# L2_ca in a four-layer cross-attention kernel: paired scores, sums of exps on GpSimd, and a later wait for them

## Chip, cores and metric

One core of a Trainium2 chip runs the whole program. The metric is device time in microseconds, the median of several runs; lower is better.

## What is computed

Four transformer layers in float32 over x (8 batches of 112 tokens, 256 channels) with a context of 8 x 375 tokens. The blocks, in order: L0 self-attention, cross-attention and a mixture of experts; L1 self-attention, MLP, cross-attention, MLP; L2 cross-attention, gated MLP, self-attention, gated MLP; L3 cross-attention with rotary positions, MLP. The change touches one of them, L2's cross-attention. It has 16 query heads and 4 key/value heads of 64 channels, and normalises queries and keys:

```python
xn = rmsnorm(x, s1)
q = einsum('btc,chd->bthd', xn, wq_c)
k = einsum('btc,chd->bthd', ctx, wk_c)
v = einsum('btc,chd->bthd', ctx, wv_c)
q, k = qk_norm(q), qk_norm(k)          # each head's row divided by its root mean square
k, v = repeat(k, 4, axis=2), repeat(v, 4, axis=2)
attn = softmax(einsum('bqhd,bkhd->bhqk', q, k) / 8)
out = einsum('bhqk,bkhd->bqhd', attn, v)
x = x + out.reshape(B, T, H * D) @ wo_c
```

## The kernel before

Each engine runs its own program; they meet at semaphores. A block is a loop over the 8 batches (`batches`: body(0), a hardware loop over 1 to 6, body(7), and body(8), which finishes what lags). While batch b's attention is computed, the same body prepares batch b+1. The order on every engine is written out by hand: `SCHEDULES["L2_ca"]` says at which of 12 steps each piece of preparation stands.

The block L2_ca (`keys_first`) puts keys on the partitions. A batch has 4 groups of 4 query heads, one group to a key/value head; the 375 keys lie in 3 chunks of 125. So there are 12 scores (`units`), each a matmul of 125 keys by 448 (4 heads x 112 queries), L873. Two key/value heads share the 128 rows of kT, and each group's queries are held twice the height, with zeros in the other head's 64 rows (`qz`, written by ScalarE in two copies with a mask, L1264). ScalarE takes exp of each score (L1277) into pT. Because keys are on the partitions, softmax's sum over keys is a matmul with ones: VectorE first adds the three chunks of a group (`add_chunks`, L1698 for the first two, L1702 for the third; 8 additions a batch), then PE multiplies by ones (L933). `weigh` handles two groups at a time, twice a batch: it waits for the sums, does 6 matmuls of exps by values (L927, side by side in two column halves) and 2 with ones. VectorE takes the reciprocal (L1707) and multiplies (L1709); PE projects (`project`, L947) once both halves are there; VectorE adds to X (L1719).

PE's pieces for the next batch, by step: 0 CT0, CT1 (context transposed); 1 XT, KP0 (keys, L816); 2 KP1; 3 QP0 (queries, L821); 4 QP1; 5 V0; 6 V1; 8 QT0 (queries transposed, L828); 9 QT1, KT1 (L835); 10 KT0. They share two PSUM banks, 7 and 5, in turn, so each waits until ScalarE has copied the piece before last. The projection uses bank 7 too and so waits for KP1's copy (L1256). `weigh` stands at step 7 (groups 0, 1) and at step 1 of the next batch (groups 2, 3), `project` at step 3. Scores rotate through 4 banks: a score waits for the exp of the score four before.

VectorE, between QP1 and QT0: the square of the queries (L1605), its sum by head (L1607), 12 small operations for reciprocal roots, the scaling of queries (L1622) and of keys (L1625), which releases QT0. The additions of chunks stand in the same queue one step behind their scores. In the last batch VectorE also computes, in small operations spread over the steps, the statistics that the next MLP needs, and after it normalises six batches of tokens (L1512). GpSimd does nothing in this block; behind it in its queue stands the splitting of weights for the MLP (`split_weights`, L2073 to L2079).

## Time and profile before

| | |
|---|---|
| median of 3 runs | 2048.26 us (2045.43 to 2050.31) |
| profiled execution, its time | 2057.58 us |
| its span | 2055.8 us |
| mean granted PE clock | 0.932 |
| PE busy | 1776.4 us, 86% |
| VectorE (DVE) busy | 1332.9 us, 65% |
| ScalarE (ACT) busy | 866.2 us, 42% |
| GpSimd (POOL) busy | 629.1 us, 31% |

A busy share is an average over 13 blocks with different limits. A float32 matmul appears as two instructions, so a score is "x2" and a pair of scores "x4". Matmuls are pipelined: the start of the next one, rather than the end of a row, tells how long PE was taken.

### The profile page before, as it was taken

To read this page: it belongs to the slowest core of one execution; us is meant where nothing else is said; L and a number is where in the kernel's file an instruction comes from. 1 tells how busy PE (TensorE), PEld (TensorE's weight loads), DVE (VectorE), ACT (ScalarE), POOL (GpSimd) and SP (SyncE) were. 2 spreads that over 40 slices of the span, in tenths; PEclk is the share of its full clock that TensorE was granted. 3 is DMA by queue.
4 is the path that set the end of the run, shared out by engine and by line. 5 is a ranking of instruction groups with operands and counts; after the bars stand their busy time and mean duration, and the time that the engine had idled before them with its cause. 6 is when DMAs were issued, how large, how long until landed. Compare 5 with 4: busy or idle time off the path is not lost.

```text
span 2055.8 us, 34270 instructions
## 1 busy us (share of the span) xinstructions
PE 1776.4 (86%) x10630; PEld 1237.2 (60%) x10630; DVE 1332.9 (65%) x3354; ACT 866.2 (42%) x2513; POOL 629.1 (31%) x732
## 2 busy tenths in 40 slices
PE   5969999769996878988779999896888979898988
PEld 4746665558985656655565555483444845455567
DVE  5866767301117876788666676796677966556665
ACT  3735554322334643565324444342332435444521
POOL 2325555210022234676320000130000325455534
PEclk9979998879998978999789999997998989999999
DMA  4100000468862000002100010101000100000200
GB/s 167 37 20 15 13 7 16 147 217 301 307 236 82 0 1 31 32 30 71 67 8 16 16 69 0 42 11 62 0 0 19 55 1 12 23 11 11 72 1 18
DMA packets 36627, 115.15 MB, mean 56 GB/s; under 512 B 2961, under 2 KB 23345, under 8 KB 29345
## 3 DMA queue, kind: packets, MB, share of 16 engines
q1 hardware_dynamic: 33968, 107.33, 15.2%
q0 software_dynamic: 2544, 6.43, 1.0%
q8 instruction: 56, 0.92, 0.2%
q14 instruction: 59, 0.48, 0.1%
HBM read 99.34 MB, written 14.40 MB: 55 GB/s over the span
## 4 chain that ended last, share of the span: by engine, by line
PE 44%; issue 20%; DVE 14%; POOL 14%; ACT 4%; DMA 3%; SPq 1%; POOLq 0%; DVEq 0%; ACTq 0%
POOL arena L2020 11%; PE ps L1008 7%; PE ps L1048 4%; PE ps L821 4%; PE ps L873 3%; PE ps L1168 3%; PE ps L1152 3%; PE ps L927 3%; PE ps L816 3%; PE ps L947 2%; PE ps L891 1%; PE ps L863 1%; DMA wml<-in_wm_L_moe 1%; PE ps L933 1%; ACT arena L1286 1%
## 5 line engine op out<-in xcount | busy, mean ns | idle before, releaser
L2020 POOL TENSOR_TENSOR arena<-arena,rinv 112x375 f32<-112x375 f32 (+1 forms) x448 | 371.1, 830 | 489.9 <-DVE rinv L1675 479.7
L891 PEld LDWEIGHTS ps<-cst,arena 112*125 112x125 f32 (+1 forms) x1408 | 188.1, 184 | 176.6 <-POOL arena L2020 88.9
L891 PE MATMUL ps<-cst,arena 112*125 112x112 f32 (+1 forms) x1408 | 247.0, 294 | 45.2 <-POOL arena L2020 39.9
L1286 ACT ACTIVATE arena<-ps,negmax 112x375 f32<-112x375 f32 (+1 forms) x384 | 190.6, 501 | 168.2 <-DVE negmax L1670 167.8
L1684 DVE COPY arena<-ps 125x336 f32<-125x336 f32 x384 | 190.8, 497 | 47.3 <-PE ps L891 44.9
L2073 POOL TENSOR_TENSOR w_split_sb<-wml,w_split_sb 128x512 fp32r<-128x512 f32 (+1 forms) x40 | 45.9, 1148 | 527.0 <-ACT w_split_sb L1352 525.1
L1670 DVE TENSOR_REDUCE negmax<-ps 112x1 f32<-112x375 f32 (+1 forms) x288 | 158.3, 550 | 70.9 <-PE ps L863 61.9
L1008 PE MATMUL ps<-h_split_sb,w_split_sb 128*128 128x448 f32 x768 | 179.7, 383 | 17.8 <-DVE h_split_sb L1559 7.1
L1286 ACT ACTIVATE arena<-arena,negmax 112x112 f32<-112x112 f32 (+1 forms) x256 | 125.4, 491 | 139.1 <-DVE negmax L1659 97.0
L1008 PEld LDWEIGHTS ps<-h_split_sb,w_split_sb 128*128 128x128 f32 x768 | 150.4, 198 | 35.9 <-DVE h_split_sb L1559 13.2
L816 PE MATMUL ps<-wat,arena 128*125 128x256 f32 (+1 forms) x608 | 153.5, 390 | 16.8 <-DVE arena L1600 9.5
L816 PEld LDWEIGHTS ps<-wat,arena 128*125 128x125 f32 (+1 forms) x608 | 110.6, 189 | 46.8 <-issue 15.4
L863 PE MATMUL ps<-arena 64*112 64x375 f32 x512 | 119.0, 543 | 19.9 <-ACT arena L1286 8.6
L873 PE MATMUL ps<-arena 128*125 128x448 f32 (+1 forms) x256 | 120.6, 560 | 11.3 <-ACT arena L1268 11.3
L947 PE MATMUL ps<-wat,arena 128*112 128x256 f32 x512 | 125.2, 389 | 4.7 <-ACT arena L1294 2.9
L1707 DVE RECIPROCAL arena<-ps 128x448 f32<-128x448 f32 x32 | 94.5, 2953 | 48.4 <-PE ps L933 48.4
L1048 PE MATMUL ps<-g_split_sb,w_split_sb 128*128 128x448 f32 x480 | 113.3, 373 | 3.2 <-DVE g_split_sb L1826 3.2
L1675 DVE RECIPROCAL rinv<-rowsum 112x1 f32<-112x1 f32 (+1 forms) x448 | 70.4, 157 | 62.5 <-PE ps L868 47.3
L821 PE MATMUL ps<-wat,arena 128*112 128x512 f32 x192 | 103.2, 675 | 6.6 <-ACT arena L1224 6.5
L947 PEld LDWEIGHTS ps<-wat,arena 128*112 128x112 f32 x512 | 87.9, 179 | 32.4 <-issue 6.3
L927 PE MATMUL ps<-arena,vz 125*64 125x448 f32 (+1 forms) x448 | 98.6, 568 | 9.6 <-DVE arena L1702 6.5
L1277 ACT ACTIVATE arena<-ps 125x448 f32<-125x448 f32 (+1 forms) x128 | 70.1, 548 | 75.1 <-PE ps L873 74.8
(221 smaller groups left out, 3186.7 us busy)
## 6 DMA issues: line engine op xcount, KB each, us to landing
wml<-in_wm_L_moe SPq DMA_DIRECT2D x21, 1028.0 KB, 7.7
wml<-in_wm_L_moe SPq DMA_DIRECT2D x21, 1024.0 KB, 7.7
craw<-in_ctx SPq DMA_DIRECT2D x40, 375.0 KB
wml<-in_wm_L_m SPq DMA_DIRECT2D x3, 3072.0 KB, 13.8
wat<-in_wa_L_ca SPq DMA_DIRECT2D x2, 2560.0 KB, 10.2
wml<-in_wm_L_m SPq DMA_DIRECT2D x2, 2048.0 KB, 10.1
keys_hbm<-arena SPq DMA_DIRECT2D x8, 375.0 KB
values_hbm<-vz SPq DMA_DIRECT2D x8, 375.0 KB
```

The source lines that it names most:

```text
L816: last = mm(ps[0:blk.kp, W_BANK, i * D:(i + 1) * D], kv[:, k2, q * blk.kp:(q + 1) * blk.kp], w[:, k2], start=k2 == 0, stop=k2 == DC - 1)
L821: last = mm(ps[0:S, W_BANK, :], hT[:, k2], wq[:, k2, i * 512:(i + 1) * 512], start=k2 == 0, stop=k2 == DC - 1)
L873: mm(ps[0:blk.kp, blk.bank_at(s), 0:HG * S], kT[:, parity(b), g // 2, q * blk.kp:(q + 1) * blk.kp], qz[:, parity(b), HG * g:HG * (g + 1)], ...
L891: last = nc.tensor.transpose(ps[0:blk.kp, T_BANK + s % blk.t_banks, o:o + S], buf[:, i * blk.nk + q * blk.kp:i * blk.nk + (q + 1) * blk.kp ...
L927: last = mm(ps[64 * z:64 * z + 64, O_BANK, 0:HG * S], vz64[0:kp, par, q, (g - 1 + z) * 64:(g + z) * 64], pT[0:kp, (g - 1 + z) % 4, q], sta ...
L947: last = mm(ps[0:S, blk.out_bank, blk.out_at:blk.out_at + D], oT[:, c], wo[:, c], start=c == 0, stop=c == blk.cq - 1)
L1008: last = mm(out, w[:, k2, v], h_split_sb[:, h, k2, tokens], start=k2 == 0 and i == 0, stop=k2 == DC - 1 and i == 2)
L1048: last = mm(ACC(c, half), w[:, c * P:(c + 1) * P], g_split_sb[:, t % 2, g], start=f == 0 and i == 0, stop=f == FC - 1 and i == 2)
L1286: last = go(probs[0:S, s % blk.nprobs, i * nk:(i + 1) * nk], src[:, i * nk:(i + 1) * nk], ACT.Exp, scale=-1.0 if blk.mask == "input" else ...
L1670: v.tensor_reduce(negmax[:, s * blk.heads:(s + 1) * blk.heads], src, AX_X, ALU.max, negate=True).then_inc(maxed, 1)
L1684: last = v.tensor_copy(pT[0:kp, place(blk, s) // gu % 4, :, place(blk, s) % HG], T_[:, 0:KC * S].rearrange("p (k s) -> p k s", s=S))
L2020: pool.tensor_tensor(p3, p3, r3, ALU.mult).then_inc(scaled, 1)
```

## The change

In L2_ca alone: scores are issued in pairs, two matmuls of 64 rows each, one in the upper and one in the lower half of PE's rows, for two groups and the same chunk. Queries are kept once, scaled by 0.125, in one ScalarE copy per transposed piece instead of two. `group_of` now orders the 12 units as (group 0, chunk 0), (group 1, chunk 0), (group 0, chunk 1) and so on. The chunk additions move from VectorE's program to GpSimd's, with the same waits. `weigh` waits for the exps of its groups before its products, and for the sums just before the matmuls with ones.

```diff
-PAIRS = ("L0_ca", "L1_ca", "L3_ca",)
+PAIRS = ("L0_ca", "L1_ca", "L2_ca", "L3_ca")
...
                     if not blk.keys_first:
                         pe.wait_ge(turned, count(st["turn"], units, b, (g + 1) * gu))
-                    elif blk.kc > 1:
-
-                        pe.wait_ge(summed, count(0, 4, b, g + 1))
                     else:
-                        pe.wait_ge(exped, count(st["unit"], units, b, g + 1))
+                        pe.wait_ge(exped, count(st["unit"], units, b, (g + 1) * gu))
...
                     if blk.keys_first:
+                        if blk.kc > 1:
+                            pe.wait_ge(summed, count(0, 4, b, g + 1))
                         for z in range(2):
...
@@ VectorE @@
-                def add_chunks(b, s):
...
-                        elif at and blk.kc > 1:
-                            add_chunks(*at)
...
@@ GpSimd @@
+                def add_chunks(b, s):
+
+                    g, q = group_of(blk, s)
+                    if q == 0:
+                        return
+                    pool.wait_ge(exped, count(st["unit"], units, b, s + 1))
+                    new = pT[0:kp, g, q].rearrange("p h s -> p (h s)")
+                    if q == 1:
+                        wait(pool, av_done, count(st["group"], 2, b, g // 2 - 1))
+                        pool.tensor_tensor(psums[0:kp, g], pT[0:kp, g, 0].rearrange("p h s -> p (h s)"), new, ALU.add)\
+                            .then_inc(part_summed, 1)
+                    else:
+                        pool.wait_ge(part_summed, count(0, 4, b, g + 1))
+                        pool.tensor_tensor(psums[0:kp, g], psums[0:kp, g], new, ALU.add).then_inc(summed, 1)
+
+                def body_of_sums(b):
+                    for s in steps(b, blk, 1):
+                        at = lagged(b, s, 1, units)
+                        if at:
+                            add_chunks(*at)
...
+                elif blk.kc > 1:
+                    batches(pool, body_of_sums)
```

The order on PE around the projection, before: the second weighing's end (L933), XT (L786), KP0 (L816), score 2 (L873), KP1 (L816), score 3, then the projection (L947).

```order
L933 MATMUL ps<-arena,cst 64x448 x2
...
L786 MATMUL ps<-cst,xn 128x112
...
L816 MATMUL ps<-wat,arena 125x256 x3
...
L873 MATMUL ps<-arena 125x448 [waits exped]
...
L816 MATMUL ps<-wat,arena 125x256 [waits w_done1,w_done0]
L816 MATMUL ps<-wat,arena 125x256
...
L873 MATMUL ps<-arena 125x448 [waits exped]
...
L947 MATMUL ps<-wat,arena 112x256 [waits w_done0]
```

And now (L932 is the matmul with ones, L858 a score, L946 the projection):

```order
L932 MATMUL ps<-arena,cst 64x448 [waits summed]
L932 MATMUL ps<-arena,cst 64x448
...
L786 MATMUL ps<-cst,xn 128x112
...
L816 MATMUL ps<-wat,arena 125x256 x3
L858 MATMUL ps<-arena 125x448 [waits exped]
L858 MATMUL ps<-arena 125x448
...
L816 MATMUL ps<-wat,arena 125x256 [waits w_done1,w_done0]
L816 MATMUL ps<-wat,arena 125x256
...
L946 MATMUL ps<-wat,arena 112x256 [waits w_done0]
```

Both scores now stand before KP1, and nothing stands between KP1 and the projection.

The order on PE at a batch's end, before: score 8, QT0 (L828), score 9, QT1, KT1 (L835), score 10, KT0, score 11.

```order
L873 MATMUL ps<-arena 125x448 [waits exped]
L828 MATMUL ps<-cst,arena 128x112 [waits qk_ready,w_done1]
L828 MATMUL ps<-cst,arena 128x112 x3
L873 MATMUL ps<-arena 125x448 [waits exped]
L828 MATMUL ps<-cst,arena 128x112 [waits out_done,w_done0]
L828 MATMUL ps<-cst,arena 128x112 x3
L835 MATMUL ps<-cst,arena 128x125 [waits w_done1]
L835 MATMUL ps<-cst,arena 128x125 x2
L873 MATMUL ps<-arena 125x448 [waits exped]
L835 MATMUL ps<-cst,arena 128x125 [waits qk_ready,out_done,w_done0]
L835 MATMUL ps<-cst,arena 128x125 x2
L873 MATMUL ps<-arena 125x448 [waits exped]
```

And now:

```order
L858 MATMUL ps<-arena 125x448 [waits exped]
L858 MATMUL ps<-arena 125x448
L828 MATMUL ps<-cst,arena 128x112 [waits qk_ready,w_done1]
L828 MATMUL ps<-cst,arena 128x112 x3
L828 MATMUL ps<-cst,arena 128x112 [waits out_done,w_done0]
L828 MATMUL ps<-cst,arena 128x112 x3
L835 MATMUL ps<-cst,arena 128x125 [waits w_done1]
L835 MATMUL ps<-cst,arena 128x125 x2
L858 MATMUL ps<-arena 125x448 [waits exped]
L858 MATMUL ps<-arena 125x448
L835 MATMUL ps<-cst,arena 128x125 [waits qk_ready,out_done,w_done0]
L835 MATMUL ps<-cst,arena 128x125 x2
```

Score 9 now stands ahead of the wait for the normalised queries (qk_ready), and score 11 ahead of KT0; no score stands between QT0 and QT1, nor after KT0.

## Rows read from the trace of the kernel before

**Rows 1.** Stretch view, one batch of L2_ca: us, then busy us (instructions), granted PE clock

```profile
core 0: us, PE busy (x) PEld busy (x) DVE busy (x) ACT busy (x) POOL busy (x), PEclk, DMA share, GB/s
1131.40:1162.40 31.00, 30.71 (x127) 16.97 (x126) 21.26 (x34) 13.76 (x29) 0.00 (x0) 1.00 0.04 13
```

**Rows 2.** Timeline around QT0, PE and ACT: start us, us, engine, line, operation

```profile
1193.73 0.60 PE L828 MATMUL ps<-cst,arena 112*128 112x112 f32 x4
...
1194.37 1.16 ACT L1264 ACTIVATE arena<-ps,cst 128x448 f32<-128x448 f32 x2
...
1195.84 1.17 ACT L1264 ACTIVATE arena<-ps,cst 128x448 f32<-128x448 f32 x2
...
1196.88 0.51 ACT L1268 ACTIVATE arena<-ps 128x375 f32<-128x375 f32 x1
...
1197.44 1.89 PE L873 MATMUL ps<-arena 128*125 128x448 f32 x4
1197.67 0.53 ACT L1268 ACTIVATE arena<-ps 128x375 f32<-128x375 f32 x1
```

**Rows 3.** Timeline from the scores after KP1 to the sixth score

```profile
1207.42 0.91 PE L873 MATMUL ps<-arena 128*125 128x448 f32 x2
...
1207.62 0.39 ACT L1256 ACTIVATE arena<-ps 125x256 f32<-125x256 f32 x1 [0.32 <-PE ps L816]
...
1208.17 3.62 PE L947 MATMUL ps<-wat,arena 128*112 128x256 f32 x16
...
1215.81 0.91 PE L873 MATMUL ps<-arena 128*125 128x448 f32 x2
```

**Rows 4.** Timeline from the batch before's sixth score, VectorE's square and sum

```profile
1184.75 0.91 PE L873 MATMUL ps<-arena 128*125 128x448 f32 x2
...
1185.59 1.23 DVE L1605 TENSOR_TENSOR arena<-arena 112x1024 f32<-112x1024 f32 x1 [1.15 <-ACT arena L1253]
...
1187.02 0.63 DVE L1702 TENSOR_TENSOR arena<-arena 125x448 f32<-125x448 f32 x1 [0.21 <-DVE arena L1605]
1187.56 1.21 DVE L1607 TENSOR_REDUCE var<-arena 112x16 f32<-112x1024 f32 x1
```

**Rows 5.** Timeline of PE in L3_ca: a pair of 64 rows

```profile
1806.70 0.89 PE L868 MATMUL ps<-arena 64*112 64x375 f32 x4
1807.52 0.58 PE L891 MATMUL ps<-cst,arena 112*125 112x112 f32 x3
```

**Rows 6.** Groups of GpSimd by form: count, busy us, mean ns, idle before

```profile
L2020 POOL TENSOR_TENSOR arena<-arena,rinv 112x448 f32<-112x448 f32 x64 | 59.7, 933 | 179.2 <-DVE rinv L1675 179.2
...
L2010 POOL TENSOR_TENSOR arena<-arena,scratch 112x512 f32<-112x512 f32 x16 | 18.5, 1156 | 0.1
```

**Rows 7.** Timeline of the last batch and the tail of L2_ca

```profile
1296.48 2.96 DVE L1707 RECIPROCAL arena<-ps 128x448 f32<-128x448 f32 x1 [2.62 <-PE ps L933]
...
1300.15 1.98 PE L947 MATMUL ps<-wat,arena 128*112 128x256 f32 x8 [0.36 <-DVE arena L1709]
...
1301.97 3.17 PE L873 MATMUL ps<-arena 128*125 128x448 f32 x8
...
1305.07 2.48 PE L927 MATMUL ps<-arena,vz 125*64 125x448 f32 x12
...
1308.23 3.27 PE L873 MATMUL ps<-arena 128*125 128x448 f32 x8
...
1312.76 1.68 POOL L2073 TENSOR_TENSOR w_split_sb<-wml,w_split_sb 128x512 fp32r<-128x512 f32 x1 [268.45 <-ACT w_split_sb L1352]
1313.24 1.23 DVE L1478 TENSOR_TENSOR newton<-rstd 112x6 f32<-112x6 f32 x1
...
1317.90 2.55 DVE L1512 TENSOR_SCALAR arena<-X,rstd 112x256 f32<-112x256 f32 x6
...
1318.03 4.14 PE L927 MATMUL ps<-arena,vz 125*64 125x448 f32 x12 [6.53 <-DVE arena L1702]
...
1322.97 2.96 DVE L1707 RECIPROCAL arena<-ps 128x448 f32<-128x448 f32 x1 [2.52 <-PE ps L933]
```

**Rows 8.** Timeline of PE in L2_sa, after an idle

```profile
1541.78 1.00 PE L873 MATMUL ps<-arena 128*112 128x448 f32 x2 [1.48 <-ACT arena L1268]
```

**Rows 9.** Stretch view, 2 us of L2_sa just behind, columns as in rows 1

```profile
1544.00:1546.00 2.00, 2.00 (x6) 0.29 (x2) 0.50 (x1) 0.00 (x0) 0.00 (x0) 0.50 0.00 0
```

More of the change, by code:

```diff
@@ L1687, in copy_turned @@
                     last.then_inc(turned, 1)
-                def add_chunks(b, s):
-                    g, q = group_of(blk, s)
-                    if q == 0:
-                        return
-                    dve.wait_ge(exped, count(st["unit"], units, b, s + 1))
-                    new = pT[0:kp, g, q].rearrange("p h s -> p (h s)")
-                    if q == 1:
-                        v.tensor_tensor(psums[0:kp, g], pT[0:kp, g, 0].rearrange("p h s -> p (h s)"), new, ALU.add)\
-                            .then_inc(part_summed, 1)
-                    else:
-                        dve.wait_ge(part_summed, count(0, 4, b, g + 1))
-                        v.tensor_tensor(psums[0:kp, g], psums[0:kp, g], new, ALU.add).then_inc(summed, 1)
                 def divide(b, p):
@@ L1984, in attention @@
                 blk, st = BLOCKS[n], START[n]
-                units, nk = blk.units, blk.nk
+                units, nk, kp = blk.units, blk.nk, blk.kp
                 q3 = qt[0:S].rearrange("p (h d) -> p h d", d=64)
```

## The prediction

> **What bounds it now.** I read the busy shares by stretch first, for the block L2_ca, which runs from about 1055 to 1329 us. One batch in its middle lasts 31 us, and PE is busy for 30.7 of them at full granted clock, DVE for 21.3, ACT for 13.8, GpSimd for none [rows 1]. So PE's own work bounds a batch, and what the change gives is the PE time it removes, up to the point where another chain is late. The period, from the sixth score of one batch to that of the next, is 1215.81 - 1184.75 = 31.06 us [rows 3, 4]. I cut it at two places where PE depends on others: the transposes of the queries (QT0), and the last second-half query projection (QP1), which ends about when the sixth score starts.
> - QT0 to the next batch's first score: QT0 starts at 1193.73. Score 11 starts at 1197.44 and the next score 0 right after ScalarE's KT0 copy, which ends at 1197.67 + 0.53 = 1198.20; with the 0.21 from copy to matmul, 1198.41: 4.68 us [rows 2].
> - First score to QP1's end: 1198.41 to 1215.81, 17.40 us [rows 2, 3].
> - QP1's end to QT0: 1184.75 to 1193.73, 8.98 us [rows 2, 4]. PE has little idle time here: the VectorE chain that normalises queries and keys (square, sum, root, two scalings) ends at the same moment as PE's own work; the stall before QT0 is 0.13 us.
>
> **The change, step by step**, against the profiled execution (2057.58 us).
>
> *Price of a pair.* A single score starts the next matmul 0.75 us after itself (score 3 at 1207.42, PE after it 0.75 later at 1208.17) [rows 3]. The block before has no pair of 64 rows over 448 columns. The nearest is L3_ca's pair over 375 columns: 1806.70 to 1807.52, 0.82 us, where 375 columns alone stream in 0.75 x 375/448 = 0.63 [rows 5]. So two matmuls run side by side, but each isolated pair costs 0.19 on top: 0.75 + 0.19 = 0.94. Bounds: 0.75 (no overhead) and 1.50 (no overlap). I take 0.94, the nearest row. The Trainium skill (TensorEngine Tiling (Array Packing), Theoretical Speedup) gives up to a factor of 2 for a contraction of at most 64; by that a pair would cost 0.75 and the sum below would be some 5 us larger.
>
> *First score to QP1's end, new.* Five single scores (3.75) become three pairs (2.82): -0.93. But score 3, which stood between KP1 and the output projection, is gone. The projection must wait for the copy of KP1 out of its bank: KP1 ends at 1207.42, the copy runs 1207.62 to 1208.01, the projection starts at 1208.17 [rows 3]. Score 3 filled these 0.75 us exactly; now they are a stall: +0.75. New: 17.40 - 0.93 + 0.75 = 17.22.
>
> *QP1's end to QT0, new.* PE's own work was 8.98 - 0.13 = 8.85; four singles (3.00) become two pairs (1.88): 7.73. The VectorE chain loses only the addition that stood between the square (ends 1186.82) and the sum of squares (starts 1187.56) [rows 4]; back to back it would start 0.03 after: -0.71, so 8.27. The later of the two decides: 8.27, with a PE stall of 0.54. The other seven additions lay in idle time of VectorE; moving them gives nothing.
>
> *QT0 to next first score, new.* From QT0 to ScalarE's first copy 0.64, then ScalarE works almost without a break to 1198.20; two of the four query copies go, each 0.52 ((1196.88 - 1195.84)/2) [rows 2]: 4.68 - 1.04 = 3.64. The pair 10, 11 ends later than single score 10 did and holds exp 10, hence the KT0 copy, by about 0.2: 3.84. This stretch is bound by ScalarE and has no room for the two scores saved.
>
> New period 17.22 + 8.27 + 3.84 = 29.33, so **-1.73 a batch**, where PE alone would have given -3.4. Six full periods lie between the seven QT0s: **-10.4**.
>
> *GpSimd's sums.* Eight additions of 125x448 a batch, both inputs in SBUF. Rows: 0.93 for 112x448 with one broadcast input, 1.16 for an addition of 112x512 [rows 6]; scaled to 448 that is 1.01, and I take 1.05 with the wait. PE now waits for exps before the products and for the sums 2.31 later (3.16 of a weighing less 0.85 of its last pair). Second weighing: additions 8 to 11 start 0.1 before QT0 and are done 5.2 after it (exp 11 ends at 4.05); the sums are wanted at 3.84 + 0.94 + 0.75 + 2.31 = 7.84. First weighing: slack some 2.8. So the new wait costs nothing as long as an addition takes under 1.9 us.
>
> *First batch.* -0.93 for three pairs, -0.71 in the VectorE chain, and two query copies fewer ahead of the first score, of which the serial transposes let about 0.5 through: **-2.1**.
>
> *Last batch.* No projections of a next batch cover anything here. From QT0 to the end of its first weighing it now takes 21.32 us (1193.73 + 3 x 31.06 = 1286.91 to 1308.23) [rows 2, 7]. New: 3.84 + 0.94 + 0.09 to the weighing, 3.16 for it, 3.86 until the divided heads are there (PE resumes at 1300.15, the reciprocal began at 1296.48, 0.19 after the weighing) [rows 7], 1.82 half a projection (to 1301.97), 0.94 for pair 4, 5, then exps 4 and 5 (1.1), 3.16: 18.9. **-2.4**.
>
> *Tail.* The dearest single thing: PE stands idle 6.5 us before its last weighing, released by the last addition [rows 7]. Exps end some 4 us after the last four scores start, but GpSimd has begun to split weights for the MLP, and VectorE's small operations, interleaved with the additions, are stretched: 1.23 for one over six numbers a row, while GpSimd's split beside it takes 1.68 [rows 7]. Each waits out the other when both read two SBUF inputs. The last reciprocal starts 14.74 after the first weighing's end (1322.97 - 1308.23). New: weighing products from about 3.1, sums by GpSimd at 1.5 + 4 x 1.05 = 5.7, ones-matmul to 6.8. But VectorE must first do its four root steps and six token normalisations (2.55) [rows 7]. It is free at 3.8, and the four steps then alternate with GpSimd's additions 10, 11 and two splits (ends 4.7, 5.85, 7.2, 7.9); the normalisations end at 10.5. Reciprocal at 10.5: **-4.2**. Bounds: without any blocking 7.4 (-7.3); with three more blockings 11.7 (-3.0). The Trainium skill (SBUF — State Buffer, Who interferes with whom) states that a VectorE operation with two SBUF inputs and a GpSimd one that reads SBUF exclude each other for a whole instruction; the stretched rows agree. Between batches only addition 5 meets such an operation, the query square; the square has begun 0.5 earlier, and what follows it is a reduction of one input.
>
> Sum: -10.4 - 2.1 - 2.4 - 4.2 = **-19.1**: 2057.58 - 19.1 = 2038.5 for the profiled execution. The median of the three runs is 2048.26, 9.3 below that execution; the same difference gives **2029.2**.
>
> **Rivals.**
> 1. *Clock falls at the new stalls (the slower side).* PE was 99% busy; now it idles 0.75 before the projection, 0.54 before QT0 and again about 1.2 until the next score. In L2_sa, after an idle of 1.48, the granted clock stood at 0.50 [rows 8, 9]; and L2_ca's last weighing, after its 6.5 idle, took 4.14 for what takes 2.48 at full clock [rows 7]. One fall costs 1.7. Against: L2_sa idles like this in every batch and nearly always keeps 1.00. Once a batch costs 7 x 1.7 = 12: 2041. It turns slower if PE works over 5.5 us of each batch at half clock (2.7 x 7 = 19.1); 8 us would give 2057. Chance 0.12, half of it slower.
> 2. *Sums come late.* If an addition takes over 1.95 the chain of four holds the second weighing, and from 2.4 on the period's gain is gone. For: rows 7 have 1.68 for a blocked GpSimd operation. Against: no pairs of two-input operations meet in additions 8 to 11. At 2.2: 1.0 of 1.73 lost in 7 batches, 2036; at 2.6, 2053. Chance 0.07.
> 3. *The pairs don't overlap*, so a pair costs 1.50. Then the period is 29.33 + 4 x 0.56 + 0.58 = 32.1, 1.1 longer than now, and with the tail's gain the whole is about 2049: no difference. Against: 0.82 in rows 5. Chance 0.05.
> 4. *More than I forecast*: pairs at 0.75 (4 on the path x 0.19 x 6 batches = 4.6) and no blocking in the tail (3.1 more), -26.8: 2021.5. Chance 0.12.
>
> The forecast keeps 0.64. Its own bounds: tail -3.0 to -7.3; the ScalarE stretch 0.3 either way in 6 batches (2); one or two clock falls (3). The range takes in most of rivals 1, 2 and 4: **2020 to 2043**. About 0.2% (4 us) is what a measurement can tell here. Faster: 0.64 + 0.12 + 0.03 of rival 1 + 0.03 of rival 2 = 0.82; same: 0.03 + 0.02 + 0.04 (rival 3) = 0.09; slower: 0.06 + 0.02 + 0.01 = 0.09.
>
> **What would show it.** A period of 29.3 between two QT0s, with idle PE ahead of the projection released by the KP1 copy, and ahead of QT0 by VectorE's key scaling; single pairs 0.94 apart from what follows; GpSimd additions near 1.0 us; no PE wait for the sums except in the tail; the gap of 6.5 before the last weighing gone, and the last reciprocal held by VectorE's own work. Wrong would be: a granted clock under 1.00 in most batches, PE released by the additions, or a QT0 stall of another size.

## The result and the profile after

The changed kernel takes 2025.76 us (median of 4 runs, 2018.84 to 2032.79) against 2049.28 (2045.43 to 2052.42): a ratio of 0.9886, 95% interval [0.9848, 0.9925], so faster by some 23 us. A second measurement gave 2024.51 against 2050.06, and 0.986 [0.9836, 0.9884]. The profiled execution took 2032.79, span 2031.0, against 2057.58 and 2055.8.

| | before | after |
|---|---|---|
| time, median | 2049.28 | 2025.76 |
| span of the profiled execution | 2055.8 | 2031.0 |
| mean granted clock | 0.932 | 0.940 |
| period of a batch in L2_ca | 31.06 | 29.75 |
| last batch, QT0 to the first weighing's end | 21.32 | 18.94 |
| tail, first weighing's end to the last reciprocal | 14.74 | 11.69 |
| L2_ca, first CT0 matmul to the issue of L2_sa's weight load | 274.01 | 258.98 |
| L2_sa: issue of L2_m2's weight load to that of L3_ca's | 184.99 | 178.60 |
| L3_ca's block (it takes in L2_m2 as well): from there to the issue of L3_m's weight load | 317.50 | 313.59 |

L2_ca lies between its first CT0 matmul (1055.83 before, 1055.09 after) and SyncE's issue of L2_sa's weight load (1329.84 and 1314.07). Of the 24.8 us between the two spans it gives 15.0. The rest lies in blocks whose instructions the change leaves alone; two experiments and a comparison over all profiles, below, are about it.

**A batch in the middle.** Stretch view of the changed kernel over one period, columns as in [rows 1].

```profile
1136.70:1166.45 29.75, 28.12 (x127) 14.42 (x128) 17.65 (x26) 12.21 (x27) 9.59 (x8) 1.00 0.05 14
```

Beside [rows 1]: GpSimd now has 8 instructions, VectorE 8 fewer, the clock still stands at 1.00. PE is busy for 28.12 of 29.75 us. It was busy 30.71 of 31.00. PE's work fell by about 2.6, the period by 1.31: the difference is new idle time.

Timeline of PE and ACT around the projection, start us, us, engine, line, operation, and in brackets the idle time and its releaser ([rows 3] of before):

```profile
1168.40 1.02 PE L858 MATMUL ps<-arena 64*125 64x448 f32 x4
1169.35 1.13 PE L816 MATMUL ps<-wat,arena 128*125 128x256 f32 x4
...
1170.52 0.38 ACT L1255 ACTIVATE arena<-ps 125x256 f32<-125x256 f32 x1 [0.52 <-PE ps L816]
...
1170.95 2.41 PE L946 MATMUL ps<-wat,arena 128*112 128x256 f32 x10 [0.47 <-ACT arena L1255]
```

KP1 to the projection takes 1.60, as when a score filled the gap; now PE waits there for ScalarE's copy. The pair takes 0.95 from its start to the next matmul. From KP0's start to the pair it is 1.83, against 1.74 to a single score before the change; KP1 behind it is 1.13 long, against 1.03 behind a score.

Timeline of the batch's end: the VectorE chain, then PE and ACT ([rows 4] and [rows 2] of before):

```profile
1179.90 1.23 DVE L1604 TENSOR_TENSOR arena<-arena 112x1024 f32<-112x1024 f32 x1 [2.36 <-ACT arena L1252]
1181.16 1.22 DVE L1606 TENSOR_REDUCE var<-arena 112x16 f32<-112x1024 f32 x1
...
1186.30 0.96 DVE L1624 TENSOR_TENSOR arena<-arena,rstd 125x768 f32<-125x768 f32 x1
...
1187.32 0.99 PE L828 MATMUL ps<-cst,arena 112*128 112x112 f32 x8 [0.25 <-DVE arena L1624]
1188.55 0.54 PE L835 MATMUL ps<-cst,arena 125*128 125x125 f32 x3 [0.25 <-ACT arena L1260]
1189.03 1.02 PE L858 MATMUL ps<-arena 64*125 64x448 f32 x4
...
1190.55 0.48 ACT L1267 ACTIVATE arena<-ps 128x375 f32<-128x375 f32 x1
...
1191.16 1.02 PE L858 MATMUL ps<-arena 64*125 64x448 f32 x4 [0.65 <-ACT arena L1267]
```

Square and sum now stand 0.03 apart, where an addition was. QT0 is released by VectorE's key scaling; the next batch's first pair, at 1191.16, by the KT0 copy: 3.84 after QT0.

**The tail**, the timeline of PE, DVE and POOL from the end of the first weighing, at 1295.53 ([rows 7] of before):

```profile
1299.48 3.67 PE L924 MATMUL ps<-arena,vz 125*64 125x448 f32 x12 [2.18 <-DVE arena L1693]
...
1299.48 1.05 DVE L1477 TENSOR_TENSOR newton<-rstd 112x6 f32<-112x6 f32 x1
1300.56 1.05 DVE L1479 SCALAR_TENSOR_TENSOR newton<-newton,var 112x6 f32<-112x6 f32 x1
1301.65 1.19 DVE L1481 SCALAR_TENSOR_TENSOR rstd<-newton,rstd 112x6 f32<-112x6 f32 x1
1302.88 4.42 DVE L1511 TENSOR_SCALAR arena<-X,rstd 112x256 f32<-112x256 f32 x6
1307.22 2.94 DVE L1691 RECIPROCAL arena<-ps 128x448 f32<-128x448 f32 x1
...
1299.38 2.21 POOL L2028 TENSOR_TENSOR arena<-arena 125x448 f32<-125x448 f32 x2
1301.56 1.26 POOL L2078 TENSOR_TENSOR w_split_sb<-wml,w_split_sb 128x512 fp32r<-128x512 f32 x1
```

The last weighing starts 3.95 after the first one's end instead of 9.8; it takes 3.67 where the ones before it take 2.48, for behind its wait of 2.18 the granted clock falls to 0.50 (1301 to 1303 us), as it did before the change. This costs nothing here, because the end is now VectorE's: three small operations take 1.05 to 1.19 each beside GpSimd's additions and its first split, and six normalisations take 4.42 where before they took 2.55.

### The profile page after: what moved, and what is told of

The parts are those of the page before. It is cut to its first block, busy times and chain, and to the rows that moved or that the text cites. A ratio compares the mean times of both kernels' runs of the same rounds, so it can differ in the third digit from the quotient of the medians.

```text
span 2031.0 us, 34257 instructions
## 1 busy us (share of the span) xinstructions
PE 1745.6 (86%) x10630; PEld 1212.1 (60%) x10630; DVE 1302.1 (64%) x3290; ACT 852.8 (42%) x2497; POOL 702.5 (35%) x796
## 4 chain that ended last, share of the span: by engine, by line
PE 41%; issue 20%; DVE 17%; POOL 14%; ACT 4%; DMA 3%; SPq 1%; POOLq 0%; DVEq 0%; ACTq 0%
POOL arena L2002 11%; PE ps L1007 7%; PE ps L1047 5%; PE ps L821 4%; PE ps L1167 3%; PE ps L1151 3%; PE ps L946 2%; PE ps L816 2%; PE ps L924 2%; PE ps L858 1%; PE ps L891 1%; PE ps L863 1%; DMA wml<-in_wm_L_moe 1%; ACT arena L1285 1%; DVE arena L1604 1%
## 5 line engine op out<-in xcount | busy, mean ns | idle before, releaser
L1007 PE MATMUL ps<-h_split_sb,w_split_sb 128*128 128x448 f32 x768 | 178.9, 381 | 17.7 <-DVE h_split_sb L1558 7.1
L1007 PEld LDWEIGHTS ps<-h_split_sb,w_split_sb 128*128 128x128 f32 x768 | 149.7, 197 | 35.9 <-DVE h_split_sb L1558 12.9
L816 PE MATMUL ps<-wat,arena 128*125 128x256 f32 (+1 forms) x608 | 154.4, 392 | 17.2 <-DVE arena L1599 9.9
L816 PEld LDWEIGHTS ps<-wat,arena 128*125 128x125 f32 (+1 forms) x608 | 109.2, 189 | 51.9 <-issue 20.1
L946 PE MATMUL ps<-wat,arena 128*112 128x256 f32 x512 | 126.7, 393 | 7.8 <-ACT arena L1293 2.9
L946 PEld LDWEIGHTS ps<-wat,arena 128*112 128x112 f32 x512 | 88.7, 181 | 35.5 <-issue 6.5
L1047 PEld LDWEIGHTS ps<-g_split_sb,w_split_sb 128*128 128x128 f32 x480 | 91.3, 192 | 15.2 <-DVE g_split_sb L1808 7.2
```

Of the source, the lines that this page charges most:

```text
L816: last = mm(ps[0:blk.kp, W_BANK, i * D:(i + 1) * D], kv[:, k2, q * blk.kp:(q + 1) * blk.kp], w[:, k2], start=k2 == 0, stop=k2 == DC - 1)
L946: last = mm(ps[0:S, blk.out_bank, blk.out_at:blk.out_at + D], oT[:, c], wo[:, c], start=c == 0, stop=c == blk.cq - 1)
L1007: last = mm(out, w[:, k2, v], h_split_sb[:, h, k2, tokens], start=k2 == 0 and i == 0, stop=k2 == DC - 1 and i == 2)
L1047: last = mm(ACC(c, half), w[:, c * P:(c + 1) * P], g_split_sb[:, t % 2, g], start=f == 0 and i == 0, stop=f == FC - 1 and i == 2)
```

## The experiments

Twelve kernels ran, among them the two kernels of the comparison once more. "Block" below is the time from VectorE's first reciprocal in L2_ca to the issue of L2_sa's weight load: 229.57 before, 216.33 after. It is taken inside one profile, so it leaves out the later blocks. A time is a median; a ratio is to the kernel before, measured beside it. The kernel before itself took 2049.5 beside pairs alone, sums alone and the two runs on the wait, 2050.1 beside the next four (the changed kernel again, the doubled additions, the extra copies, the early KP1) and 2055.1 beside the rest, so medians from the last group look some 5 us too long next to the others.

### The changed kernel again

> The changed kernel once more, timed in five rounds against the kernel before, and a second profile of it. From the profiles the block L2_ca itself gives 13 to 16 us; the other 8 to 9 us of the profiled difference lie in blocks that the change doesn't touch (6.4 in L2_sa), where the granted clock differed. Theory (those are the clock's chance): with more runs the difference shrinks towards 16 us, and the second profile has the period of 29.75 again but other times for L2_sa. Rival (the blocks behind gain by the change): 22 us or more again, L2_sa near 179 us again.

2024.51 us, ratio 0.986 [0.9836, 0.9884]. Period 29.75, block 216.30. What L2_ca does repeats to 0.03 us. L2_sa took 179.38, L3_ca's block 310.23. The theory (the difference shrinks towards 16) failed: it is 25.6 between the medians, and the rival's two signs came. The last two sections on the experiments ask which part of that is chance.

### Pairs alone

Additions back in VectorE's program, and PE waits for the sums ahead of the products again; pairs and query copies as changed.

```diff
+                    elif blk.kc > 1:
+                        pe.wait_ge(summed, count(0, 4, b, g + 1))
...
-                        if blk.kc > 1:
-                            pe.wait_ge(summed, count(0, 4, b, g + 1))
...
+                        elif at and blk.kc > 1:
+                            add_chunks(*at)
...
-                elif blk.kc > 1:
-                    batches(pool, body_of_sums)
```

> Pairs and single queries as in the change; the additions stay on VectorE and the wait for the sums stays ahead of the products. Theory (a batch is a cycle of PE, the VectorE chain before QT0 and ScalarE's copies): the addition between square and sum is back (+0.7 on the 29.75 of the changed kernel), and the four additions of the batch's end, which stand behind the reciprocal, are done about 6.0 us after QT0, while PE would be at the weighing 5.6 after it: +0.5 to +1.2. Period 31.0 to 31.6 us, no better than the 31.06 of before; the 6.5 us gap of the tail stays; total within 3 us of before. Rival (PE's own work is the bound and the pairs are the gain): period 29.8 to 30.2 and 8 us or more faster than before.

2046.6 us, ratio 0.9979 [0.9966, 0.9993]; period 30.88, block 230.04. Waits of PE in 120 us of L2_ca, in us in total, times, longest:

```profile
PE ps L828 <- DVE arena L1624: 3.9, 4, 1.0
PE ps L858 <- ACT arena L1267: 2.0, 3, 0.7
PE ps L946 <- ACT arena L1255: 1.9, 4, 0.5
PE ps L926 <- DVE arena L1701: 1.4, 4, 0.3
```

The pairs on their own give 0.18 of a period. The stall before QT0 is 1.0 instead of 0.25: the addition between the square and the sum holds the chain, 0.7 as the prediction had it. The second weighing waits another 0.3 for the additions. Together 1.1, the distance from 30.88 to 29.75. The period is just under the 31.0 to 31.6 expected. In the tail the gap before the last weighing did not stay at 6.5, it grew to 8.88, and the last two reciprocals lie 16.57 apart instead of 14.56; that takes back what the period gives, so the block is no shorter. PE's saving cannot come out as long as VectorE still adds.

### GpSimd's sums alone

Changed kernel without the pairs, wait ahead of the products.

```diff
-PAIRS = ("L0_ca", "L1_ca", "L2_ca", "L3_ca")
+PAIRS = ("L0_ca", "L1_ca", "L3_ca",)
```

> The additions on GpSimd alone: single scores, queries held twice, wait ahead of the products. Theory: a batch is bound by PE's own 30.9 us, so the period falls only from 31.06 to about 30.9; the tail gains some 3 us (the last weighing no longer waits for VectorE's queue, and the last reciprocal is then held by VectorE's normalisations); last batch about the same. Total 4 us faster than before, plus or minus 2. Rival (moving the sums is the main gain): period under 30.3, 8 us or more faster.

2041.57 us, ratio 0.9957 [0.9941, 0.9973]; period 31.31, block 228.79. In L2_ca this edit gives 0.8 us: the tail is 3.5 shorter between the last two reciprocals, but the last batch is longer by 1.3 and the period by 0.25 (30.9 was expected). The timeline of PE, VectorE and GpSimd ahead of QT0 shows the reason:

```profile
1193.13 1.02 PE L873 MATMUL ps<-arena 128*125 128x448 f32 x2
1194.27 0.61 PE L828 MATMUL ps<-cst,arena 112*128 112x112 f32 x4
...
1190.80 1.16 DVE L1481 SCALAR_TENSOR_TENSOR rstd<-newton,rstd 125x28 f32<-125x28 f32 x1
...
1190.78 1.13 POOL L2024 TENSOR_TENSOR arena<-arena 125x448 f32<-125x448 f32 x1 [2.69 <-ACT arena L1276]
```

QT0 starts 1.14 after score 8 instead of 0.88. With single scores an addition of GpSimd starts 0.02 before the last small root step, which takes 1.16 instead of 0.19. That is more than the 0.7 which the chain gains by losing its own addition. It happens in all six periods (1.04 to 1.16), and in no period of the changed kernel, where the additions start at other times. Yet the whole is 8 us shorter. That gain lies outside L2_ca; see the section on VectorE's stalls. The 4 us expected were too few by it, and the rival's period under 30.3 did not come.

### The late wait alone, and the change without it

The kernel before with PE's wait for the sums moved behind the products:

```diff
-                    elif blk.kc > 1:
-                        pe.wait_ge(summed, count(0, 4, b, g + 1))
...
+                        if blk.kc > 1:
+                            pe.wait_ge(summed, count(0, 4, b, g + 1))
```

> The kernel before with one edit: PE waits for the sums after the six products. Theory: middle batches unchanged (sums come 0.9 us ahead of the weighing there), period 31.06; last batch 0.7 to 1.3 us shorter; tail: the last products no longer wait, the matmul with ones follows VectorE's last addition at once, and the last reciprocal starts 2.5 us earlier. Total 3 to 4 us faster than before. Rival (the gap in the tail is the dearest thing and a later wait removes it): 6 us or more faster.

2046.4 us, ratio 0.9986 [0.9969, 1.0003]; period 31.06, block 227.59. The wait alone gives nothing in a period, nor the 0.7 to 1.3 expected in the last batch (21.32 again), and 2.0 at the end; PE then waits at the ones matmul. Timeline of its tail:

```profile
1307.21 2.48 PE L924 MATMUL ps<-arena,vz 125*64 125x448 f32 x12 [0.68 <-ACT arena L1276]
1313.08 0.97 PE L932 MATMUL ps<-arena,cst 125*64 125x448 f32 x4 [3.39 <-DVE arena L1701]
```

The changed kernel with the wait ahead of the products (the same two pieces the other way round):

> The changed kernel with the wait for the sums back ahead of the products. Theory: in a middle batch the last addition ends 0.25 us after PE reaches the second weighing, so +0.3 a batch; in the last batch +0.9 and +1.9; the tail unchanged, since VectorE's normalisations hold the last reciprocal. Total +4 to +5 us on the changed kernel. Rival (the late wait matters only in the tail): period unchanged at 29.75, total within 2 us of the changed kernel.

2039.12 us, ratio 0.9933 [0.9911, 0.9955]; period 30.03 to 30.10, block 221.05. The timeline shows where, in a batch, in the last batch and in the tail:

```profile
1191.01 2.48 PE L926 MATMUL ps<-arena,vz 125*64 125x448 f32 x12 [0.28 <-POOL arena L2028]
...
1293.90 2.48 PE L926 MATMUL ps<-arena,vz 125*64 125x448 f32 x12 [2.17 <-POOL arena L2028]
...
1303.17 4.17 PE L926 MATMUL ps<-arena,vz 125*64 125x448 f32 x12 [4.34 <-POOL arena L2028]
```

So the late wait is worth 0.3 a period and 2.8 in the last batch (0.95 up to the first reciprocal after QT0, 1.85 more up to the next, as expected), and about 5 in the block. The 4.34 in the tail costs nothing: the last two reciprocals lie 11.51 apart with and without it, since VectorE's normalisations hold the last one. But the whole is longer by much more than the 4 to 5 expected: the ratios 0.9933 and 0.986 differ by some 15 us. The other 10 us are in no stretch that these profiles can hold against the edit; L2_sa took 184.76 in this profile and 179.38 in that of the changed kernel, and the next-to-last experiment is about such differences. It stays open.

### Each addition twice

Each of GpSimd's additions is preceded by a second one that writes to an unused place (one of the two pieces shown).

```diff
+                        pool.tensor_tensor(ms[0:kp, g % 2], psums[0:kp, g], new, ALU.add)
                         pool.tensor_tensor(psums[0:kp, g], psums[0:kp, g], new, ALU.add).then_inc(summed, 1)
```

> The changed kernel; each GpSimd addition of L2_ca is done twice, the first time into an unused tile, so twice the work ahead of the sums (2.3 us for one). Theory: four such at the batch's end start 0.5 after QT0 and are done at 9.7, while the matmul with ones is wanted at 7.9: +1.8; the query square on VectorE is blocked by the fourth-last addition for about 0.5: +0.5. Period 31.5 to 32.3, total 12 to 18 us slower than the changed kernel. Rival (the late wait leaves enough room): period under 30.3.

2051.68 us, ratio 0.9992 [0.997, 1.0014]; period 31.49, block 235.66. Timeline of PE at QT0 and in the weighing, and VectorE's square:

```profile
1189.52 1.46 DVE L1604 TENSOR_TENSOR arena<-arena 112x1024 f32<-112x1024 f32 x1 [2.36 <-ACT arena L1252]
...
1197.85 0.99 PE L828 MATMUL ps<-cst,arena 112*128 112x112 f32 x8 [1.15 <-DVE arena L1624]
...
1206.55 0.97 PE L932 MATMUL ps<-arena,cst 125*64 125x448 f32 x4 [0.64 <-POOL arena L2030]
```

At 2.26 an addition (two of 1.13) the ones matmul waits 0.6 for the sums, and the VectorE chain, met by more GpSimd work, costs 0.9 more before QT0: 1.74 a batch. This is rival 2 made real: the new wait has slack at 1.13 and none at 2.26, and the whole gain of the period goes. The 31.49 holds for four of the six periods; the other two take 33.5. In these the granted clock falls behind a wait at QT0, of 3.10 in the first period and of 1.15 in the third. In the third, shown here, the matmuls from 1168.0 to 1172.6 run at 0.50, and a pair takes 1.86 of busy time instead of 1.02:

```profile
1164.38 0.99 PE L828 MATMUL ps<-cst,arena 112*128 112x112 f32 x8 [1.15 <-DVE arena L1624]
...
1169.33 1.86 PE L858 MATMUL ps<-arena 64*125 64x448 f32 x4 [0.65 <-ACT arena L1267]
```

The next three periods have the same waits and keep 1.00. So rival 1, too, comes near once the stalls grow, at 2.0 a fall. The whole is 27 us slower than the changed kernel, not the 12 to 18 expected; the block has 19.3 of them.

### Two more query copies a batch

ScalarE copies each half of the transposed queries a second time, to an unused place.

```diff
+                        if blk.name == "L2_ca":
+                            go(ms[:, i], W[:, 0:4 * S], ACT.Identity, scale=0.125)
```

> The changed kernel; ScalarE copies each transposed query piece once more, into an unused tile, as often as before the change. Theory (the stretch from QT0 to the next first score is bound by ScalarE): period +0.9 to +1.05, to 30.65 to 30.8, all of it in that stretch; total 6 to 8 us slower than the changed kernel. Rival (PE or the wait for the pair's second score bounds the stretch): +0.3 or less.

2027.36 us, ratio 0.9871 [0.9839, 0.9903]; period 30.19, block 219.35. 0.84 us of ScalarE's work (0.42 from start to start, twice) makes the period 0.44 longer, where 0.9 to 1.05 was expected. PE's wait ahead of KT1 grows from 0.25 to 0.69, and the wait ahead of the next batch's first pair stays 0.65:

```profile
1186.84 0.54 PE L835 MATMUL ps<-cst,arena 125*128 125x125 f32 x3 [0.69 <-ACT arena L1262]
...
1189.45 1.02 PE L858 MATMUL ps<-arena 64*125 64x448 f32 x4 [0.65 <-ACT arena L1269]
```

So one of two copies lies on the path, the first; the second falls into a gap of 0.33 that ScalarE has before the exp of this stretch. The change itself moved the KT1 copy from 3.15 to 1.92 after QT0, by 1.23 and not by 1.04, because the two copies left take 0.42 to 0.44 from start to start and not 0.52 each. But from the KT1 copy to the KT0 copy it is now 1.31 instead of 0.79: the gap of 0.33 is ScalarE waiting for the pair 10, 11.

### KP1 one step earlier

```diff
-        plan={0: ["CT0", "CT1"], 1: ["XT", "KP0"], 2: ["KP1"], 3: ["QP0"], 4: ["QP1"], 5: ["V0"], 6: ["V1"],
+        plan={0: ["CT0", "CT1"], 1: ["XT", "KP0", "KP1"], 3: ["QP0"], 4: ["QP1"], 5: ["V0"], 6: ["V1"],
```

> The changed kernel with the piece KP1 one step earlier, ahead of scores 2 and 3, so that these cover its copy out of the bank that the projection needs. Theory (score 3 had filled that wait): PE's idle 0.47 before the projection is gone, period 29.2 to 29.35, total 3 to 4 us faster than the changed kernel. Rival (another wait takes its place: the copy now stands ahead of exps 2 and 3, or QT0's wait on VectorE grows): period within 0.15 of 29.75.

2022.38 us, ratio 0.9859 [0.9834, 0.9885]; period 29.01, block 212.06. A pair now stands between KP1 and the projection, and the projection waits for nothing:

```profile
1162.45 2.77 PE L816 MATMUL ps<-wat,arena 128*125 128x256 f32 x12
1165.15 1.02 PE L858 MATMUL ps<-arena 64*125 64x448 f32 x4
1166.10 3.71 PE L946 MATMUL ps<-wat,arena 128*112 128x256 f32 x16
```

The period falls by 0.74, the stall that the prediction had priced at 0.75. The 29.2 to 29.35 expected was the profile's idle of 0.47 alone; KP1 to the projection had taken 1.60, where KP1 to a score takes 0.86.

### Weights split later

GpSimd splits the weights of L2_m1 only when three pairs of token groups are normalised.

```diff
+                if BLOCKS[n].name == "L2_m1":
+                    pool.wait_ge(xn_ready, START[n]["xn"] + SOON)
                 split_weights(n)
```

> The changed kernel, but GpSimd begins to split the weights of the next block (L2_m1) only when VectorE has normalised the tokens of three of that block's six token groups, not as soon as the weights have arrived. Theory (the tail gives less than forecast because VectorE's small operations and GpSimd's splits, both reading two SBUF inputs, exclude each other): the six normalisations take about 2.6 us as before the change, not 4.4, the root steps keep only the stretch that additions 10 and 11 give them, and the last reciprocal comes 2 to 3 us earlier after the first weighing's end than the 11.7 of the changed kernel, at about 9; the first matmul of L2_m1 comes 1 to 3 us earlier, the whole 2 us shorter (2023). Period unchanged at 29.75. Rival (the normalisations are stretched by GpSimd's additions, or by waits on TensorE, not by the splits): the last reciprocal stays at 11.5 or more. Rival 2 (the splits themselves are then late for L2_m1): its first matmul comes later than in the changed kernel and the whole is 0 to 5 us longer.

2026.91 us, ratio 0.9871 [0.9852, 0.9891]; period 29.75. Timeline of VectorE in its tail, and the first split on POOL:

```profile
1290.80 1.06 DVE L1477 TENSOR_TENSOR newton<-rstd 112x6 f32<-112x6 f32 x1
1291.89 1.05 DVE L1479 SCALAR_TENSOR_TENSOR newton<-newton,var 112x6 f32<-112x6 f32 x1
1292.97 0.17 DVE L1481 SCALAR_TENSOR_TENSOR rstd<-newton,rstd 112x6 f32<-112x6 f32 x1
1293.17 1.67 DVE L1511 TENSOR_SCALAR arena<-X,rstd 112x256 f32<-112x256 f32 x6
1295.75 2.96 DVE L1691 RECIPROCAL arena<-ps 128x448 f32<-128x448 f32 x1 [0.91 <-PE ps L932]
...
1294.97 1.27 POOL L2078 TENSOR_TENSOR w_split_sb<-wml,w_split_sb 128x512 fp32r<-128x512 f32 x1 [2.06 <-issue]
```

The six normalisations take 1.67 with no GpSimd instruction beside them, 4.42 with splits. (The 2.06 of idle time ahead of the first split is the new wait, which the profile puts down to nothing.) Two root steps are still stretched, by the two additions that run beside them. The last reciprocal starts 8.9 after the first weighing's end instead of 11.7, and the block is 2.4 shorter (213.97). The first weight matmul of L2_m1 (L1007) comes 33.9 after the last QT0 instead of 36.3, so rival 2 did not come. In the ratio this gain can't be seen: 0.9871 lies between the changed kernel's two results.

### Both edits, and two pairs in a row

> The changed kernel with both edits: KP1 runs at step 1, directly behind KP0 (so that a pair of scores stands between it and the output projection), and the split waits as in the run with the later split. Theory: the two lie in different stretches, so they add up: period 29.0 as with the early KP1 alone, tail 9 instead of 11.7; L2_sa's load is issued 5 + 2 us earlier than in the changed kernel, at about 1305; the whole 2016 to 2020. Rival (what one gives the other takes): the sum is no better than the early KP1 alone, about 2022.

Both edits: 2024.04 us, ratio 0.9857 [0.9836, 0.9879]; period 29.01, the tail as in the last run, block 209.52. The two gains add up: 6.8 off the block, against 4.3 and 2.4 alone. The whole time shows no gain over the early KP1 alone (0.9859) and misses the 2016 to 2020 expected.

The third one on top of both:

```diff
-        plan={0: ["CT0", "CT1"], 1: ["XT", "KP0", "KP1"], 3: ["QP0"], 4: ["QP1"], 5: ["V0"], 6: ["V1"],
+        plan={0: ["CT0", "CT1"], 1: ["XT", "KP0", "KP1"], 3: ["QP0", "QP1"], 6: ["V0", "V1"],
```

> As the run before, and the second-half query projection QP1 stands directly behind QP0, so that the score pairs 4, 5 and 6, 7 run one behind the other, and both value projections follow them. Theory A (what a pair costs beyond one score is paid where TensorE goes over to 64-row matmuls and back, 0.19 behind and 0.09 ahead, not in each pair; in the last batch two pairs in a row take 1.77 of busy time where one takes 1.02): the four matmuls take 1.77, TensorE has 0.28 less to do, QP1 ends 0.9 earlier, so the VectorE chain is no longer last at QT0, and the period falls from 29.0 to about 28.5; L2_sa's load is issued some 3.5 us earlier than in the run before. Theory B (the cost is each pair's own): the period falls only by the 0.26 stall ahead of QT0, to 28.75. Rival (score 4 to 7 close together wait for exps to free a bank, or the first weighing waits for the sums of these scores, which now come later): a new idle ahead of the weighing, period 29.0 or more.

2020.59 us, ratio 0.9834 [0.9817, 0.985], the best of all; period 28.53, block 206.65.

```profile
1169.15 1.77 PE L858 MATMUL ps<-arena 64*125 64x448 f32 x8
1170.85 2.85 PE L816 MATMUL ps<-wat,arena 128*125 128x256 f32 x12
```

Two pairs in a row start the next matmul 1.70 after themselves, that is 0.95 + 0.75. The second pair costs what a single score does. From QP0's start to the first weighing PE needs 8.01 (1165.62 to 1173.63), where it needed 8.40 with the pairs apart (1169.64 to 1178.04 with the early KP1): 0.39 less, with the same matmuls. The overhead is paid at each turn from 128-row matmuls to 64-row ones and back, not in each pair: theory A, which forecast 28.5. It had the size of a turn at 0.28; the 0.39 are 0.20 in the pair, 0.09 ahead of it and 0.10 in the matmuls behind. VectorE's chain is still last at QT0, by 0.16 instead of 0.26, and these 0.10 with the 0.39 make up the 0.48 of the period. No wait for exps or sums came in its place.

### The kernel before again

> The kernel before, profiled once more. The changed kernel's profile was 24.8 us shorter than that of before, but only 16 of it up to L2_ca's end; 6.4 came in L2_sa and the rest in L3, whose code is the same in both. Theory (the time of these later blocks varies from one execution to the next with the granted clock, whatever the kernel; L2_sa took 178 to 185 in the nine profiles so far): here L2_sa takes a value in that span at random, and L2_ca's period is 31.06 and the load of L2_sa is issued within 3 us of 1330. Rival (the change speeds the later blocks up): L2_sa takes 185 and the blocks from L2_sa to the end over 718 us again.

2051.24 us (one run). Period 31.06, block 230.06, L2_sa's load issued at 1326.30, a little more than the 3 us from 1330 that were expected. L2_sa took 180.69, where the first profile of the same kernel had 184.99 and the changed kernel 178.60 and 179.38. Over all 14 profiles L2_sa took 178.3 to 185.0, without regard to the edit (181 with pairs alone, 178 with the sums alone, 185 with the early KP1 and with each addition twice). It goes with the mean granted clock of this stretch: 0.93 in the eight of at most 180.7, 0.91 in the one of 183.0, 0.89 in the five from 184.7 on. So the 6.4 us by which L2_sa was shorter in the compared profiles are for the most part one execution's luck with the clock. From L2_sa's load to the issue of the output, the kernel before took 717.8 this time, not 720.6; the changed kernel 711.6 and 708.0. The gap didn't close: part of it is the edit's.

### VectorE's stalls in L3_ca, over all profiles

The part that doesn't go by chance is L3_ca's block. It took 317.1 to 318.6 us in the four profiles in which VectorE's program holds the additions (before, twice; pairs alone; late wait alone) and 310.2 to 313.6 in the ten in which GpSimd's does: no overlap, means of 317.8 and 311.3. (The block includes L2_m2, but the stalls below are both in L3_ca.) L3_ca doesn't use these additions. Its row for VectorE's row-sum reciprocal, in the view of groups over that block, for before and then for the changed kernel (count, busy us, mean ns, idle time ahead and what ended it):

```profile
L1675 DVE RECIPROCAL rinv<-rowsum 112x1 f32<-112x1 f32 x94 | 14.9, 159 | 51.3 <-PE ps L868 41.9 <-issue 6.5 <-DVE arena L1639 1.0
```

```profile
L1674 DVE RECIPROCAL rinv<-rowsum 112x1 f32<-112x1 f32 x94 | 14.9, 158 | 46.8 <-PE ps L868 43.8 <-DVE arena L1636 1.0 <-DVE arena L1638 1.0
```

6.5 us of VectorE's idle time end with nothing that it waited for ("issue"), in two pieces. The first, in the timeline of before, with the PE wait that follows from it, and the traffic of 5 us around it by DMA queue (packets, MB, share):

```profile
1790.29 0.17 DVE L1675 RECIPROCAL rinv<-rowsum 112x1 f32<-112x1 f32 x1 [3.17 <-issue]
...
1791.66 0.41 PE L786 MATMUL ps<-cst,xn 112*128 112x112 f32 x2 [2.95 <-DVE xn L1512]
...
q14 instruction: 3, 0.02, 2.0%
```

In these 5 us a queue that the profile calls "instruction" moves three packets. That VectorE stands still because its instructions are being loaded is my reading of this. PE idles 2.95, and the granted clock of the 8 us behind is 0.79, a mixture of 2.4 and 1.2 GHz. The second piece, 3.31, comes 79 us later. The same pair of stalls, of 3.0 to 3.4 each, is in all four kernels with the additions in VectorE's program, and in none of the other ten. The page's count of packets on that queue divides them in the same way: pairs alone, then sums alone:

```profile
q14 instruction: 58, 0.48, 0.1%
```

```profile
q14 instruction: 49, 0.40, 0.1%
```

49 or 50 in all ten, 58 or 59 in all four. In L3_ca's block it is 17 before and 9 in the changed kernel. The change takes the additions out of VectorE's program ahead of L3_ca (3290 instructions run instead of 3354), and without them L3_ca's loop lies differently in it. The Trainium skill (Runtime: NRT & Kernel Launch, Instruction fetch mechanics) says that instructions come in blocks of 16 KiB, that an engine holds two, and that a jump to a block it no longer holds stalls it for a load. The traces fit the last point, with 3.2 us for a stall; the block sizes no run here shows. That it is the position and not something else I infer from 4 profiles against 10. The programs of PE and ScalarE are excluded, since pairs alone changes them and keeps the stalls. GpSimd's program is not: it takes the additions in the same ten kernels. A run that changes the length of VectorE's program alone wasn't made.

## Why the prediction was right, and where not

The direction, the price of most steps and the range held; 2029.2 was forecast for the median, 2025.76 and 2024.51 came. But the sum reached its place with two errors that offset each other: in L2_ca the change gives 15.0 us, not 19.1, and outside it about 7 more came that the sum did not have. That the whole landed so near is therefore partly luck.

- **First score to QP1's end**: forecast 17.22, measured 17.65 (1161.42 to 1179.07, one period before the pair at 1191.16). The failed term is the pair's price. I took 0.94 from L3_ca's pair [rows 5], the time from its start to the next one's. That was 0.95 here. But an isolated pair also costs 0.09 ahead of it (KP0 to the pair 1.83 instead of 1.74, QP0 to the pair 1.81 instead of 1.72) and about 0.10 in the group behind (QP1 1.81 instead of 1.71; KP1 too, but there the stall hides it). So it costs 1.13 or 1.14, and these three and the 0.01 of each pair make 0.31 of the 0.43. Another 0.09 comes from the stall: the projection takes 3.55 from its start to QP0 instead of 3.46, and stands behind the wait, not behind a pair. The two rows of [rows 5] hold one of three parts. The next step, that the filling score before the projection is lost and costs 0.75, came out to the hundredth: moving KP1 gave 0.74 back.
- **QP1's end to QT0**: forecast 8.27, measured 8.25, held by VectorE's chain. The stall at QT0 is 0.32 rather than 0.54, counted as the prediction counts it, from 0.95 after the pair's start (the profile's row has 0.25), since PE's own work came to 7.93 instead of 7.73 under that cover. Pairs alone shows the other half of the step: with the addition in the chain, 0.7 more.
- **QT0 to the next first score**: forecast 3.84, measured 3.84. Three errors cancelled here, which is luck: the copies gave 1.23 and not 1.04, the pair 10, 11 took back 0.52 and not 0.2, and from the KT0 copy's start to the score it is 0.61 and not 0.74.
- **Period**: 29.75, not 29.33; from the second QT0 to the eighth 178.62 instead of 186.34, so -7.7 instead of -10.4. Some three quarters of the miss is the term of the pair, and most of the rest the projection behind the stall.
- **GpSimd's addition**: forecast 1.05, measured 1.13, below the 1.16 of [rows 6]. The sums are in time between batches, as forecast; each addition twice crossed the threshold and took the gain, as rival 2 says.
- **First batch**: -1.4 to the first QT0 and -0.45 to the second, against -2.1. The -1.4 is not the change's: KP0 and KP1 are the same matmuls in both, but their row took 4.88 before and 3.40 after. In the second profile of the kernel before, the first QT0 comes as early as in the changed kernel (17.30 and 17.20 after the first CT0), the second one 27.07 later instead of 25.68, and the two together give -1.5. **Last batch**: 18.94, forecast 18.9.
- **Tail**: -3.05, forecast -4.2, the bound with more blockings -3.0. The step that failed is "at the normalisations' end 10.5": I had the normalisations at the 2.55 of [rows 7], a row that already held some blocking. They took 4.42 beside the splits and 1.67 without; the root steps were done at 7.35 instead of 7.9, which made up for some of it.
- **Rival 1**, a fall of the clock at the new stalls, did not come: the clock stays at 1.00 in the middle of L2_ca with idle pieces of 0.25 to 0.65 us. Its argument against, that L2_sa nearly always keeps 1.00 with such idles, misreads the trace of before: there the clock is 0.58 to 0.74 in 1480 to 1490 and 1575 to 1585 us and 0.50 in 1545 to 1550. The doubled additions show one such fall, behind a wait of 1.15. **Rival 3** did not come: a pair is 1.13 in all, not 1.50. **Rival 4** did not come either: a pair costs 1.13 and not 0.75, and the tail is blocked; its 2021.5 is about as far from the two medians as the forecast.
- **What the sum lacked**: VectorE's two stalls in L3_ca, loads of instructions as I read them. Six and a half us, more than half of what the six periods in L2_ca gave, stood in the trace of before as two idle pieces without a releaser, 450 us after the block that I read. I looked only at stretches whose instructions the change touches. With it the parts come nearer to the medians: block -13.2, up to the first reciprocal -1.8, L3_ca -6.5 make -21.5, against -23.5 and -25.6 measured; for the sums alone -0.8 and -6.5 against -8.0; for the last version -22.9, -2 and -6.5 against -34.5. With the wait ahead of the products they overshoot: -8.5, -1.3 and -6.5 against -10.4. So up to 6 us either way remain to the clock's chance and unexplained.

## What to carry to other kernels

When work moves from a chain that ends last to an idle engine, the gain is what the chain that ends last loses, not the busy time of the work; and look for what the moved work will run beside, for one addition beside one small root step cost more than the chain had gained. When matmuls are merged, ask which wait each one filled: a plan that kept the old slots gave away 0.74 a batch, and moving one projection brought it back. Put 64-row matmuls next to each other, for the overhead is paid at the turn. Search the trace for idle pieces with no releaser on an engine whose program gets shorter or longer: they can come or go far from the edit.

## What the runs showed of the hardware

- A pair of 64-row matmuls over 448 columns costs 1.13 us when it stands alone between 128-row matmuls (0.95 from its start, 0.09 ahead, 0.09 or 0.10 in what follows), a second pair right behind it 0.75. A single 128-row one costs 0.75.
- In the run with doubled additions, five of six periods have waits of 1.14 to 1.28 us before QT0 and of 0.25 and 0.65 after it. The granted clock fell to 0.50 behind them in one, which was 2.0 us longer for it, and stayed at 1.00 in four.
- A small VectorE operation that reads two SBUF inputs (125x28) took 1.16 us instead of 0.19 when a GpSimd addition of 1.13 had started 0.02 before it.
- A VectorE operation with one large SBUF input, in this form (a row scaled by one number a partition, 112x256), is stretched too beside GpSimd's splits: 0.28 us each alone, 0.74 beside them. The Trainium skill (SBUF — State Buffer, Who interferes with whom) gives two ways in which VectorE contends with GpSimd: two SBUF inputs, or a mode that takes both ports for one tensor, which it says tensor_scalar can enter. The trace agrees that this tensor_scalar is held up; which of the two ways it is, no run here shows.
- VectorE can stand still for 3.2 us in the middle of a loop with nothing that it waits for, while an instruction queue moves one to three packets. It did so in the four profiles with the additions in its program and in none of the ten without, though these run 450 us earlier. One such stall of VectorE and the PE idle of 2.95 behind it were followed by a granted clock of 0.79 over 8 us.
- The time of a block whose instructions don't change (L2_sa) varied from 178.3 to 185.0 us from one profiled execution to another, with its mean granted clock from 0.93 down to 0.89. A difference below some 7 us between two single profiles says nothing until it is placed.
